# GpSimd's split of the experts' down weights, one tile sooner inside a feed-forward stage

## The chip, the cores and the metric

The program runs on one core of a Trainium2 chip. The metric is the device time of one execution in microseconds, as the median of a few runs; the profile is that of one execution. PE is TensorE, DVE VectorE, ACT ScalarE, POOL GpSimd and SP the engine that here issues transfers.

## The reference, cut to what matters

Input x is 8 x 256 x 512. Four blocks follow each other, each added to x: a convolution with 8-wide heads, a feed-forward block with quantised activations and ternary weights, an attention over a context, and a mixture of 16 experts (two routed per token) with two shared ones. The change touches the second block's stage:

```
def _bitlinear(x, w, b):
    xn = _layer_norm(x)
    xq = _activation_quant(xn)          # round(x * 127 / max|x|), per row
    wq = _weight_quant(w)               # -1, 0, 1 times a scale
    return einsum('bsd,fd->bsf', xq, wq) + b
h = _bitlinear(x, w1, b1)               # 512 -> 2048
h = gelu(h, approximate=False)
return _bitlinear(h, w2, b2)            # 2048 -> 512
```

It also touches a piece of preparation for the fourth block: that block's down weights `L1_ffn_rw2` (16 experts, 256 x 512 float32) are used as two bf16 parts, a high part (the value rounded to bf16) and a low part (the float32 difference to it).

## The kernel before, in words

The program is a row of stages; inside a stage each engine has its own instruction stream and the streams meet at semaphores. A stage ends for all engines together. The feed-forward stage is `stage_ffn` (L784). It takes 16 tiles of 128 tokens through a pipeline; every engine runs steps n = -3 ... 17, and different parts of a step belong to different tiles.

- PE, `up` (L1087): for tile t 16 matmuls of 512 columns into `ps_fH`, and four for the bias; `down` (L1111): 16 matmuls into `ps_fY`, once the transposed rounded rows (`f_qbT`) are there.
- ACT: `gelu` (L1000) reads `ps_fH` in two halves into `f_h`; `square` (L1010) sums squares and forms the variance; `scale` (L1018) multiplies by the quantiser.
- DVE: `centre` (L916) subtracts the mean (L919, 128 x 2048), `farthest` (L921) takes the largest magnitude (L923), `scale_of` (L925) needs that and the inverse root (L929 to L932), `round_h` (L934) rounds to bf16 (L938) and raises `qb_ready`, `add_y` (L942) adds the projected tile to the residual (L946). It also quantises the tile three further on (L605, L606). At the end it forms the low parts of keys and values for the next stage (L951, L955, L960), between the last two additions.
- SP, L884 to L891: for each e from 0 to 15 in program order: transpose of the quantised input of tile e + 3 (`turn_qa`, L871), transpose of the rounded rows of tile e (`turn_qb`, L877), wait for expert e's low part, store its two parts to DRAM (L889), load the raw weights of expert e + 2 (L851, 512 KB, waits that buffer e % 2 was split). The first two loads go out at the stage's start. A DMA waiting at the head of SP's stream holds back those behind it.
- POOL, L1066 to L1076: one inverse root for 12 tiles' input scales (L578), then the inverse root of tile 0 (`inverse_root`, L1050, L1052, one column). After that a loop over n: wait until tile n is rounded, cast expert n's weights to bf16 (`down_high`, L1059; waits for its load and for the store of expert n - 2, which used the same buffer), inverse root of tile n + 1, the difference for expert n (`down_low`, L1064), and for the last four n a bias addition on one tile of the residual (`add_bias2`, L1048, for tiles 0 to 3).

All orders are written out by hand; there is no planner. The four functions of POOL that are named here use no PSUM. The stored parts are read again only in the fourth block, hundreds of microseconds later.

Of the kernel before, what the change touches and what calls it, by code (L numbers as in the profile page):

```python
# [18 lines left out]
NT = TOK // P  # L19
# [764 lines left out]
def stage_ffn(k, scales, b1_parts, b2, ahead, quantised):  # L784
# [3 lines left out]
    with ExitStack() as ctx:  # L788
# [23 lines left out]
        rstd_ready, centred, quant_ready, h_scaled, qb_ready = (sem(n) for n in ("rstd", "cent", "quant", "hsc", "qb"))  # L812
# [229 lines left out]
        @block.gpsimd  # L1042
        def _(pool):
            pool.memset(ahead.rows[:, :], 0.0).then_inc(rows_zeroed, 1)

            def add_bias2(t):
                pool.wait_ge(y_added, t + 2)
                pool.tensor_tensor(tile(t), tile(t), b2[:, :].unsqueeze(1), ALU.add)  # L1048

            def inverse_root(t):  # L1050
                pool.wait_ge(var_ready, t + 1)
                pool.tensor_tensor(col(t % 2, RSTD), col(t % 2, VAR), k.pow_half[:, 0:1], ALU.pow).then_inc(rstd_ready, 1)  # L1052

            def down_high(e):
                p = e % 2
                pool.wait_ge(d_loaded[p], 16 * (e // 2 + 1))
                if e >= 2:
                    pool.wait_ge(d_stored[p], 16 * (e // 2))
                pool.tensor_copy(d_parts[p][:, 0, :], d_raw[p][:, :]).then_inc(d_high, 1)  # L1059

            def down_low(e):
                p = e % 2
                pool.wait_ge(d_high, e + 1)
                pool.tensor_tensor(d_parts[p][:, 1, :], d_raw[p][:, :], d_parts[p][:, 0, :], ALU.subtract).then_inc(d_low, 1)  # L1064

            pool.wait_ge(others_var, 1)  # L1066
            scales.inverse_root(k, pool, OTHER_TILES).then_inc(others_rstd, 1)
            inverse_root(0)
            for n in range(NT):
                pool.wait_ge(qb_ready, n + 1)  # L1070
                down_high(n)
                if n + 1 < NT:
                    inverse_root(n + 1)
                down_low(n)
                if n >= NT - AHEAD * TPB:
                    add_bias2(n - (NT - AHEAD * TPB))  # L1076
# [1993 lines left out]
```

## Time and profile before

| what | value |
|---|---|
| median of 3 runs | 1163.91 us (1163.27 to 1166.69) |
| profiled execution | 1166.8 us, its span 1165.1 us |
| mean granted TensorE clock of the span | 0.94 |
| PE busy | 1051.7 us (90%) |
| DVE busy | 881.9 us (76%) |
| ACT busy | 697.4 us (60%) |
| POOL busy | 603.2 us (52%) |
| feed-forward stage | from 230.25 us to about 371.0 us of the span |

A busy time is the time in which the engine worked on some instruction. Timeline lines give start, duration, engine, line, operation, tiles written and read, and in square brackets how long the engine had been idle and what ended that. PEld is the loading of weights into TensorE, SPq the issuing of a transfer on SP's queue. A DMA's landing is later than its issue.

### The profile page before, as it was taken

How to read it: one execution, taken by the hardware profiler on the slowest of the kernel's cores; microseconds unless marked ns; L12 is line 12 of the kernel's file. 1: busy time of each engine (PE TensorE's matmuls, PEld its weight loads, DVE VectorE, ACT ScalarE, POOL GpSimd, SP SyncE). 2: the span in 40 equal slices, each digit the busy share in tenths (PEclk: the TensorE clock that was granted, in tenths of full speed). 3: DMA queues.
4: the chain of work that ended last, by engine and by line, in shares of the span. 5: the costliest groups of instructions: out<-in, count | busy, mean ns of one | idle time of the engine just before them, and what ended most of it. 6: DMA issues, size and time to landing. Idle time of an engine off the chain costs nothing. (4 is left out here: it accounts for less than half of the span.)

```text
span 1165.1 us, 24953 instructions
## 1 busy us (share of the span) xinstructions
PE 1051.7 (90%) x9247; PEld 781.0 (67%) x9247; DVE 881.9 (76%) x1610; ACT 697.4 (60%) x1135; POOL 603.2 (52%) x637
## 2 busy tenths in 40 slices
PE   5899997689997899778999989698997899999995
PEld 5677776534444567456777766497774788888883
DVE  5589998879998987667888888588966555555538
ACT  4564772889985556367888876385444354454530
POOL 4444446334454733357888887313685355555510
PEclk9999998799999999978999999658999899999998
DMA  8573531879886013222222220385796477778878
GB/s 312 191 253 110 167 101 41 157 212 227 223 223 186 24 61 109 83 63 56 56 56 57 56 56 2 108 332 184 194 267 229 160 235 241 242 233 286 318 269 302
DMA packets 133819, 194.63 MB, mean 167 GB/s; under 512 B 68102, under 2 KB 70316, under 8 KB 132904
## 3 DMA queue, kind: packets, MB, share of 16 engines
q1 hardware_dynamic: 117368, 149.45, 42.3%
q0 software_dynamic: 8544, 24.68, 6.9%
q10 hardware_dynamic: 7792, 18.96, 5.1%
q8 instruction: 72, 1.18, 0.4%
q14 instruction: 43, 0.35, 0.1%
HBM read 127.47 MB, written 44.48 MB: 148 GB/s over the span
## 5 line engine op out<-in xcount | busy, mean ns | idle before, releaser
L470 PE MATMUL ps_y<-kv,toep 128*128 128x288 f32 x640 | 156.7, 407 | 3.4 <-DMA toep<-taps_padded 2.3
L470 PEld LDWEIGHTS ps_y<-kv,toep 128*128 128x128 f32 x640 | 121.1, 190 | 38.4 <-DMA toep<-taps_padded 4.1
L1679 POOL TENSOR_TENSOR vw<-at_pf,kw 128x1024 bf16<-128x1024 f32 x64 | 136.4, 2132 | 2.7 <-ACT kw L1739 2.7
L164 POOL TENSOR_TENSOR kv<-kx 128x1024 f32<-128x1024 f32 x32 | 60.6, 1893 | 84.2 <-DVE outT L524 37.8
L2665 POOL DMA_INDIRECT expert_results<-e_yo,target x47 | 69.8, 1484 | 55.5 <-ACT e_yo L2712 55.5
L1735 ACT ACTIVATE at_pf<-ps_st 128x1024 f32<-128x1024 f32 x64 | 65.5, 1023 | 39.4 <-PE ps_st L1875 35.7
L1786 DVE TENSOR_REDUCE at_negmax<-ps_s 128x4 f32<-128x1024 f32 x64 | 78.4, 1225 | 2.5 <-PE ps_s L1836 0.6
L1147 PEld LDWEIGHTS ps_eg<-e_xT,e_w 128*128 128x128 bf16 x1128 | 69.0, 100 | 14.9 <-DVE e_w L2766 2.5
L1147 PE MATMUL ps_eg<-e_xT,e_w 128*128 128x128 bf16 x1128 | 73.1, 223 | 4.0 <-DVE e_xT L2773 4.0
L1147 PE MATMUL ps_eu<-e_xT,e_w 128*128 128x128 bf16 x1128 | 72.3, 222 | 0.0
L2766 DVE COPY e_w<-expert_weights 128x4096 bf16 x47 | 57.7, 1227 | 18.4 <-issue 18.4
L2779 DVE SCALAR_TENSOR_TENSOR e_y<-ps_eu,e_bias,e_y 128x128 f32<-128x128 f32 x94 | 28.7, 347 | 54.8 <-PE ps_eu L1147 54.1
L2660 POOL DMA_INDIRECT e_rows<-token_rows,token x45 | 43.5, 968 | 51.1 <-PE ps_ex L2866 45.2
L1739 ACT ACTIVATE kw<-at_pf 128x1024 bf16<-128x1024 f32 x64 | 67.6, 1057 | 2.0
L1100 PE MATMUL ps_fH<-w1T,f_qaT 128*128 128x512 bf16 x256 | 63.7, 393 | 3.8 <-PEq L636 2.3
L1147 PEld LDWEIGHTS ps_eu<-e_xT,e_w 128*128 128x128 bf16 x1128 | 66.6, 99 | 0.0
L1780 DVE COPY qs<-ps_m 32x256 bf16<-32x256 bf16 x128 | 37.6, 293 | 36.8 <-PE ps_m L1848 33.8
L1116 PE MATMUL ps_fY<-w2T,f_qbT 128*128 128x512 bf16 x256 | 59.4, 387 | 4.2 <-DMA f_qbT<-f_qb 4.2
L2728 ACT ACTIVATE e_xT<-ps_ex 128x512 bf16<-128x512 bf16 x47 | 28.1, 597 | 58.0 <-PE ps_ex L2866 58.0
L494 DVE TENSOR_TENSOR prod<-ps_y,qx 128x1024 f32<-128x1024 f32 x32 | 39.2, 1224 | 23.1 <-ACT ps_y L417 23.1
L1147 PE MATMUL ps_ed<-e_parts,e_yhi 128*128 128x512 bf16 x188 | 55.9, 379 | 0.4 <-DVE e_ylo L2787 0.4
L2721 ACT ACTIVATE e_y<-ps_eg,e_bias 128x128 f32<-128x128 f32 x94 | 29.4, 363 | 40.3 <-PE ps_eg L1147 31.9
(444 smaller groups left out, 3052.8 us busy)
## 6 DMA issues: line engine op xcount, KB each, us to landing
e_parts<-down_parts SPq DMA_DIRECT2D x47, 512.0 KB, 4.5
w_raw<-in_L_ffn_w ACTq DMA_DIRECT2D x32, 512.0 KB, 4.4
toep<-taps_padded SPq DMA_DIRECT2D x32, 256.0 KB, 3.5
f_draw<-in_L_ffn_rw SPq DMA_DIRECT2D x16, 512.0 KB, 4.6
down_parts<-f_dparts SPq DMA_DIRECT2D x16, 512.0 KB, 2.9
expert_weights<-expert_results SPq DMA_DIRECT2D x16, 512.0 KB, 9.6
x_res<-in_x SPq DMA_DIRECT2D x4, 1024.0 KB, 11.3
c_in<-in_ctx SPq DMA_DIRECT2D x4, 1024.0 KB, 14.3
```

The source lines that it names most:

```text
L164: pool.tensor_tensor(pairs[:, :, :, 0:HD0], x[:, :, 0:HD0].unsqueeze(2).broadcast_to([P, ROWS_N, WIDE, HD0]), sliding_rows(x, 0, 1, WIDE), ...
L470: last = pe.matmul(y[:, l * B:(l + 1) * B, :, WIDE - 1:], toep[h % 2][:, (DC - 1 - l + m) * P:(DC - l + m) * P], kv[h % 2][:, m * B:(m + 1 ...
L1100: pe.matmul(psH[:, f, :].rearrange("p (a t) -> p a t", t=P), qaT[p][:, c, :], k.w1T[:, f * DC:(f + 1) * DC, c, :], start=(c == 0), stop=False)
L1116: last = pe.matmul(psY[p][:, :].rearrange("p (a t) -> p a t", t=P), qbT[p][:, c, :], k.w2T[:, :, c, :], start=(c == 0), stop=(c == FC - 1))
L1147: instruction = pe.matmul(out, stationary[a], moving[b], start=first and n == 0, stop=last and n == 2)
L1679: pool.tensor_tensor(pl[u % 4][:, :, :, :], pf[u % 2][:, :, :, :], ph[u % 4][:, :, :, :], ALU.subtract)\
L1735: act.activation(pf[u % 2][:, :, :, :], psT[:, :, :, :], ACT.Exp, scale=SCORE_SCALE).then_inc(exped, 1)
L1739: act.activation(ph[u % 4][:, :, :, :], pf[u % 2][:, :, :, :], ACT.Copy).then_inc(p_high, 1)
L1786: dve.tensor_reduce(negmax[u % 2][:, :].rearrange("p (j q) -> p j q", j=2), psS[:, :, :, :], AX.X, ALU.max, negate=True).then_inc(max_read, 1)
L2660: pool.indirect_dma_start(out=rows[j % 2], out_offset=None, in_=k.scratch["rows"], in_offset=bass.IndirectOffsetOnAxis(ap=token[:, j:j + 1 ...
L2665: pool.indirect_dma_start(out=k.scratch["results"], out_offset=bass.IndirectOffsetOnAxis(ap=target[:, j:j + 1], axis=0), in_=yo[j % 2], in ...
L2766: dve.tensor_copy(w1[j % 2][:, :, :, :].rearrange("p h c f -> p (h c f)"), W[:, bass.ds(e, 1), :, :, :].rearrange("p o h c f -> p (o h c f ...
```

## The change

The first split (cast and difference of expert 0) is placed directly behind the inverse root of tile 0, with no wait for a rounded tile. The loop runs over n from 1; round n waits for tile n - 1 to be rounded, casts expert n, takes the inverse root of tile n and forms the difference of expert n. The bias additions keep their condition on n. SP's order is not touched.

```diff
             inverse_root(0)
-            for n in range(NT):
-                pool.wait_ge(qb_ready, n + 1)
+            down_high(0)
+            down_low(0)
+            for n in range(1, NT):
+                pool.wait_ge(qb_ready, n)
                 down_high(n)
-                if n + 1 < NT:
-                    inverse_root(n + 1)
+                inverse_root(n)
                 down_low(n)
                 if n >= NT - AHEAD * TPB:
                     add_bias2(n - (NT - AHEAD * TPB))
```

NT is 16 and AHEAD * TPB is 4.

## Rows read from the trace of the kernel before

**Rows 1.** Engine time by stretch: stretch, length, busy per engine, PEclk, DMA share, GB/s.
```profile
277.00:300.00 23.00, 23.00 (x108) 10.40 (x107) 22.02 (x35) 20.88 (x28) 10.90 (x9) 1.00 0.92 225
360.20:363.50 3.30, 3.30 (x10) 1.15 (x8) 3.30 (x3) 3.30 (x4) 2.48 (x2) 0.50 0.52 110
```

**Rows 2.** Timeline of TensorE's weight loads: first group of two successive tiles.
```profile
274.24 1.61 PEld L1100 LDWEIGHTS ps_fH<-w1T,f_qaT 128*128 128x128 bf16 x8
...
282.01 1.61 PEld L1100 LDWEIGHTS ps_fH<-w1T,f_qaT 128*128 128x128 bf16 x8
```

**Rows 3.** Timeline: rounding of two successive tiles, and a GELU that waits.
```profile
269.69 1.22 DVE L938 TENSOR_SCALAR f_qb<-f_h 128x2048 bf16<-128x2048 f32 x1
...
277.18 1.22 DVE L938 TENSOR_SCALAR f_qb<-f_h 128x2048 bf16<-128x2048 f32 x1
...
317.86 1.12 ACT L1007 ACTIVATE f_h<-ps_fH,f_sc 128x1024 f32<-128x1024 f32 x1 [0.35 <-PE ps_fH L1107]
```

**Rows 4.** SP's queue in one tile, the loads' landing, and DMA idle time.
```profile
L877 SPq DMA_TRANSPOSE f_qbT<-f_qb x16: 1516/1948/3358, 249.2 to 360.9; - x16
...
278.42 2.47 SPq L877 DMA_TRANSPOSE f_qbT<-f_qb  x1
282.12 0.34 SPq L889 DMA_DIRECT2D down_parts<-f_dparts  x1
282.52 0.43 SPq L851 DMA_DIRECT2D f_draw<-in_L_ffn_rw  x1
...
DMA to landing us min/median/max: 3.6/4.6/5.8
...
289.80:290.10 0.30, 0.30 (x3) 0.18 (x2) 0.30 (x1) 0.30 (x1) 0.00 (x0) 1.00 0.01 1
```

**Rows 5.** Timeline: GpSimd's round and VectorE's scale and centring beside it.
```profile
272.47 2.13 POOL L1064 TENSOR_TENSOR f_dparts<-f_draw,f_dparts 128x1024 bf16<-128x1024 f32 x1
...
274.08 1.60 DVE L919 TENSOR_SCALAR f_h<-f_h,f_sc 128x2048 f32<-128x2048 f32 x1
...
278.46 1.04 POOL L1059 CAST f_dparts<-f_draw 128x1024 bf16<-128x1024 f32 x1 [3.86 <-DVE f_qb L938]
...
279.46 0.54 POOL L1052 TENSOR_TENSOR f_sc<-f_sc,pow_half 128x1 f32<-128x1 f32 x1
...
280.63 0.21 DVE L929 TENSOR_SCALAR f_sc<-f_sc 128x1 f32<-128x1 f32 x1
...
281.89 1.29 DVE L919 TENSOR_SCALAR f_h<-f_h,f_sc 128x2048 f32<-128x2048 f32 x1
```

**Rows 6.** Timeline: GpSimd's first two casts.
```profile
249.14 1.04 POOL L1059 CAST f_dparts<-f_draw 128x1024 bf16<-128x1024 f32 x1 [6.88 <-DVE f_qb L938]
...
255.98 1.04 POOL L1059 CAST f_dparts<-f_draw 128x1024 bf16<-128x1024 f32 x1 [3.20 <-DVE f_qb L938]
```

**Rows 7.** Timeline: centrings without and with a bias addition beside them.
```profile
331.19 1.04 POOL L1059 CAST f_dparts<-f_draw 128x1024 bf16<-128x1024 f32 x1 [4.13 <-DVE f_qb L938]
...
334.90 1.29 DVE L919 TENSOR_SCALAR f_h<-f_h,f_sc 128x2048 f32<-128x2048 f32 x1
...
342.56 1.27 POOL L1048 TENSOR_TENSOR x_res<-x_res,ffn_b 128x512 f32<-128x512 f32 x1
342.68 2.24 DVE L919 TENSOR_SCALAR f_h<-f_h,f_sc 128x2048 f32<-128x2048 f32 x1
```

**Rows 8.** Timeline of the stage's end: TensorE's last projections, VectorE's last work.
```profile
358.99 5.30 PE L1116 MATMUL ps_fY<-w2T,f_qbT 128*128 128x512 bf16 x16 [3.15 <-DMA f_qbT<-f_qb]
...
360.79 1.22 DVE L951 TENSOR_TENSOR kv_c0lo<-ctxT,kv_c0hi 128x1024 bf16<-128x1024 f32 x1
361.93 2.06 DVE L955 TENSOR_TENSOR kw<-qs,kw 128x1024 bf16<-128x1024 f32 x1
...
365.33 3.61 PE L1116 MATMUL ps_fY<-w2T,f_qbT 128*128 128x512 bf16 x16 [1.04 <-DMA f_qbT<-f_qb]
...
366.97 3.35 DVE L960 TENSOR_TENSOR vw<-qs,vw 128x2048 bf16<-128x2048 f32 x1
...
370.25 0.74 DVE L946 SCALAR_TENSOR_TENSOR x_res<-ps_fY,f_out_scale,x_res 128x512 f32<-128x512 f32 x1
```

## The prediction

> **What bounds the kernel now.** I read the page first (the whole program keeps TensorE busy for nine tenths of its span), then the table of engine time by stretch for the feed-forward stage, which runs from 230 to 371 us, then the timeline of single tiles engine by engine, with SP's queue last. In the body of the stage TensorE has no gap at all and VectorE is busy 22.0 of 23 us, while GpSimd has only 10.9 of 23 [rows 1]. So GpSimd is not a bound in itself; what can matter is when its small inverse root comes, what its long operations do to VectorE, and when the transfers behind it run.
>
> Two clocks run side by side. TensorE starts the first matmul group of a tile every 282.01 - 274.24 = 7.77 us [rows 2]. The VectorE and ScalarE chain rounds a tile every 277.18 - 269.69 = 7.49 us [rows 3]. The chain is thus the faster one by 0.28 us a tile; it begins the stage behind and catches up, and the first row in which ScalarE waits for TensorE's projection (0.35 us) is at 317.86 [rows 3]. From there TensorE sets the pace, and four more tiles follow until 350 us. A delay of the chain is forgiven up to about 4 x 0.28 = 1.1 us, and what is more arrives in the tail. The tail (from 350 us) is one tile's latency: centring, maximum, scale, rounding, the transposing DMA, the last down-projection 365.33 to 368.94, and the last add, 370.25 to 370.99 [rows 8].
>
> **The change part by part.** GpSimd's instructions stay the same in number, so I ask only what moves.
>
> 1. The first split. GpSimd idles for 6.88 us ahead of 249.14, so from 242.26 [rows 6]. The cast (1.04 us) and the difference (2.13 us) [rows 5] fit: 3.17 us, done by about 245.5. Expert 0's load was issued at the stage's start. VectorE has little but columns of one element in that time. Cost 0; the next root is due only after 249 us. If the cover were gone the price would be at most these 3.17 us.
>
> 2. The body. The n-th round now waits for the rounding of tile n - 1, which is the event that released the round before it, and issues cast, root, difference in the same order. Root n therefore hangs on the same event as before. Only the expert's number is one higher. Nothing is gained: the root ends at 279.46 + 0.54 = 280.00 and VectorE's first use is at 280.63, behind its own reduction [rows 5], so 0.6 us of slack were already there.
>
> 3. The transfers. SP takes, for each tile, the transposing DMA of the rounded rows, then the store of the split weights, then the load of the expert two further on. Before, the store waited for GpSimd: issued at 282.12, and the load at 282.52, which is 3.70 and 4.10 us behind the transpose's issue at 278.42 [rows 4]. Now the split is done a tile earlier, so store and load follow the transpose's own issue (median 1.95, at most 3.36 us). But the load's consumer comes a whole tile sooner: load e + 2, issued behind transpose e, is wanted when tile e + 1 is rounded, 7.49 + 0.04 = 7.53 us after transpose e was issued. Before, it was wanted 15.0 us after. The landing: issue to landing is 3.6/4.6/5.8 us [rows 4]. If nothing queues, it lands 1.95 + 0.4 + 4.6 = 7.0 us after the transpose's issue, 0.5 us in time. If the DMA engines are the limit, only their idle gap ahead of the store can be won; it is 0.6 us (289.80 to 290.40, share 0.01 in the first half [rows 4]), so 4.10 + 4.6 - 0.6 = 8.1 us, 0.6 us late. If nothing is won, 8.7, which is 1.2 us late. I take 7.8: the engines are busy for 0.92 of the time [rows 1], so nearer to the queued case. That is 0.3 us late.
>
> The Trainium skill's page "DMA: Bandwidth & Descriptors", section "Queues, rings and completion order", says that on each DMA engine descriptors are consumed in ring order, so an earlier store only queues behind the transpose; by that rule the landing would be the 8.1 us case and the sum below about 1 us larger. The idle gap of 0.6 us is what the trace shows of it; no row shows a store queued.
>
> What 0.3 us costs: the root has 0.6 us of slack, so nothing there. But GpSimd's difference then ends 0.3 us later and lies longer over VectorE's centring. Where it overlaps that by 0.5 us (272.47 + 2.13 = 274.60 against a start at 274.08) the centring takes 1.60 us, where it overlaps by 0.2 us 1.29 [rows 5]. So 0.3 us for a late tile; as landings scatter to both sides I take half, 0.15 us a tile, for 11 tiles 1.65 us. The first such load is worse: the interval from 249.14 to 255.98 is only 6.84 us [rows 6], so it is 0.9 us late, of which 0.6 is hidden; with the overlap I take 0.6 us. Sum 2.25, less the 1.1 forgiven: **+1.15 us** in the tail. Bounds: 0 (all land in time), and rival B below.
>
> 4. The bias adds. They hang on n >= 12, so each of the four comes one tile sooner: three before lie beside a later tile's work and one at the very end; now one lands behind the difference of the round that starts at 331.19, from about 334.8 to 336.1. VectorE's centring at 334.90 takes 1.29 us today; the next one, which meets a bias add at 342.56, takes 2.24 us [rows 7]. So +0.95 us on VectorE, once, and only part of ScalarE's later waits for TensorE (0.35 to 0.8 us) takes it up, because GpSimd's own work moves with the chain and overlaps the two next centrings longer. I carry it as **+0.9 us**; bounds 0 and 1.4.
>
> The Trainium skill's page "SBUF — State Buffer", section "Who interferes with whom", says that GpSimd and a VectorE operation in a two-port mode exclude each other for the whole instruction; by that rule the centring would wait for 336.1 and cost 1.2 us in place of 0.95. The row at 342.68 agrees in kind.
>
> 5. The tail. After the last rounding (360.87) GpSimd had a cast, a difference and a bias add; all are gone. VectorE's two key differences took 2.06 us each, its value difference 3.35, while the batch's difference of the same size as a key half took 1.22 just before [rows 8]. Uncontended I put them at 1.2, 1.2 and 2.3 (twice the elements). The last add then no longer waits behind the value difference (370.32) but for TensorE's end at 368.94: 369.0 + 0.74 = 369.7 against 370.99, **-1.27 us**. The first key half's gain goes nowhere, as the add after it waits for TensorE at 364.3. The last store goes out earlier and was not last anyway. All engines pass into the next stage at this end, and TensorE starts there at once, so a shift of the end is passed on.
>
> The sum: +1.15 + 0.9 - 1.27 = +0.8 us. The profiled execution took 1166.8 us (span 1165.1, 1.7 around it), 2.9 above the median of the three runs, so it would become 1167.6, and the median 1163.9 + 0.8 = **1164.7 us**.
>
> **Rivals.** About 0.3%, or 3.5 us, is what a measurement of this kernel tells from no change.
>
> A, all hidden: loads land in time, and the chain's waits absorb the extra bias add. For it: ScalarE waits for TensorE in the last body tiles. Against: VectorE's 22.0 of 23 us. Then only the tail counts: 1163.9 - 1.3 = 1162.6 us.
>
> B, slower: the loads set the pace. The place is the cast that waits for a load in each round; the price is that cast, root and difference all shift, and the centring waits them out. It decides once a load lands more than 0.6 us late at the 7.49 us cycle. With the landing at 8.7 us the cycle P settles where the delay equals the lateness: P = 7.49 + (8.7 - P), so 8.1 us, 0.6 more for each of 12 tiles, 7.2 us. Less 1.1, plus 0.9, minus 1.3: +5.7, 1169.6 us. For it: the load's landing of up to 5.8 us. Against: its issue surely comes sooner, and the engines do have a gap.
>
> C, the clock: the down-projection of tile 14 ran from 358.99 for 5.30 us, the last for 3.61 [rows 8], with a granted clock of 0.50 from 360.20 to 363.50 [rows 1], after TensorE had starved for 3.15 us. If the shifted tail puts both down-projections into the low stretch: +0.8 + 1.7 = 1166.4; if neither, about 1163.0.
>
> D, the change does not do what it says: it does split sooner, but nobody waits for the split but the store, so this coincides with the forecast.
>
> **Chances.** Forecast 0.48 (own range 1163.4 to 1166.3), A 0.24, B 0.16, C 0.12. Only an unforeseen shift in the later stages gives over 3.5 us of gain. Faster 0.08, within 0.74, slower 0.18 (B and a bad C). The range for 8 in 10 is 1161.9 to 1168.6.
>
> **What would show it.** In the changed profile: a cast near 242.3 us and none behind the last rounding; the casts of the body waiting for the load's DMA instead of the rounded tile, and loads issued about 2.4 us behind the transpose; centrings around 1.4 to 1.6 us, and one near 335 us at 2.2; VectorE's value difference at 2.3 us and the last add set free by TensorE. The step on transfers is wrong if no cast waits for a DMA; the step on bias adds if the end of the last centring is not later relative to the stage's start; the forecast as a whole if the stage's length changes by over 2.5 us.

## The result and the profile after

The changed kernel is slower: 1171.86 us (median of 8 runs, 1169.63 to 1176.4) against 1164.55 us for the kernel before on the same chips (8 runs, 1162.93 to 1168.75). The ratio is 1.0054, 95% interval 1.0035 to 1.0072, so +6.3 us (+4.1 to +8.4). It lies above the forecast range; the rival with the load as pacemaker, which I had put at 0.16, is what happened, at about its price (+5.7).

The page of the kernel after, its opening lines and the clock (the span of before was 1165.1 us, its POOL busy time 603.2):

```profile
span 1169.1 us, 24952 instructions
## 1 busy us (share of the span) xinstructions
PE 1055.2 (90%) x9247; PEld 778.4 (67%) x9247; DVE 884.6 (76%) x1610; ACT 698.0 (60%) x1135; POOL 602.3 (52%) x637
...
PEclk9999998799998999978999999758999899999998
```

The instructions are the same and GpSimd's busy time did not grow, so somebody waits. The stage is measured from its first load's issue to the first load of the next stage: 371.26 - 230.25 = 141.0 us before, 376.74 - 229.25 = 147.5 us after. These 6.5 us are the size of the whole loss, and what GpSimd waited for tells where they arise. (The two profiled spans differ by 4.0 us only: outside the stage this execution of the changed kernel was 2.5 us shorter.) The waits of the kernel after in the stage (engine and line, releaser, us in total, times, longest), the loads' landing times, and the engine times of a stretch that answers to [rows 1]:

```profile
POOL f_dparts L1059 <- DMA f_draw<-in_L_ffn_rw: 37.1, 9, 5.5
POOL f_dparts L1059 <- DVE f_qb L938: 21.7, 6, 3.9
```

```profile
DMA to landing us min/median/max: 3.8/5.2/6.0
```

```profile
276.00:299.00 23.00, 22.47 (x105) 9.85 (x102) 21.68 (x33) 19.00 (x24) 10.32 (x9) 1.00 0.79 202
```

Nine of GpSimd's casts now end their wait with the load, none did before. Loads land 5.2 us after their issue in place of 4.6 [rows 4]. TensorE, without a gap in this part before, has one (22.47 of 23 us).

One tile of it in SP's queue, on GpSimd and on VectorE, kernel after:

```profile
265.16 1.77 SPq L877 DMA_TRANSPOSE f_qbT<-f_qb  x1
266.98 1.15 SPq L889 DMA_DIRECT2D down_parts<-f_dparts  x1
268.18 0.44 SPq L851 DMA_DIRECT2D f_draw<-in_L_ffn_rw  x1
...
272.65 2.52 SPq L877 DMA_TRANSPOSE f_qbT<-f_qb  x1
275.22 0.57 SPq L889 DMA_DIRECT2D down_parts<-f_dparts  x1
275.85 0.43 SPq L851 DMA_DIRECT2D f_draw<-in_L_ffn_rw  x1
```

```profile
274.33 1.04 POOL L1059 CAST f_dparts<-f_draw 128x1024 bf16<-128x1024 f32 x1 [5.49 <-DMA f_draw<-in_L_ffn_rw]
275.32 0.54 POOL L1052 TENSOR_TENSOR f_sc<-f_sc,pow_half 128x1 f32<-128x1 f32 x1
275.82 2.13 POOL L1064 TENSOR_TENSOR f_dparts<-f_draw,f_dparts 128x1024 bf16<-128x1024 f32 x1
281.82 1.04 POOL L1059 CAST f_dparts<-f_draw 128x1024 bf16<-128x1024 f32 x1 [3.86 <-DVE f_qb L938]
```

```profile
271.41 1.22 DVE L938 TENSOR_SCALAR f_qb<-f_h 128x2048 bf16<-128x2048 f32 x1
...
275.99 0.21 DVE L929 TENSOR_SCALAR f_sc<-f_sc 128x1 f32<-128x1 f32 x1 [1.17 <-POOL f_sc L1052]
...
276.93 2.11 DVE L919 TENSOR_SCALAR f_h<-f_h,f_sc 128x2048 f32<-128x2048 f32 x1
280.54 1.22 DVE L938 TENSOR_SCALAR f_qb<-f_h 128x2048 bf16<-128x2048 f32 x1
...
285.25 1.29 DVE L919 TENSOR_SCALAR f_h<-f_h,f_sc 128x2048 f32<-128x2048 f32 x1
288.03 1.22 DVE L938 TENSOR_SCALAR f_qb<-f_h 128x2048 bf16<-128x2048 f32 x1
```

Read it from the top. The load went out 268.18 - 265.16 = 3.0 us behind its transpose (4.1 before [rows 4]; I expected 2.4) and the cast began 9.2 us behind the transpose, while the rounding that releases the cast when the load is there was over at 272.63. So the cast is 1.6 us late, the root with it, and VectorE has nothing to do for 1.17 us at L929, where its slack had been 0.6 us [rows 5]. The difference then ends at 277.95, over the centring, which takes 2.11 us in place of 1.3. Together the cycle from rounding to rounding is 9.13 us. The next one is 7.49 us again: the long cycle gave the next load time. This tile is the worst but one: over the nine casts that waited for their load, the cast is 0.2 to 2.0 us late, 1.0 in the median, and begins 7.7 to 9.2 us behind the transpose, 8.6 in the median. The stage goes on mostly in such pairs, and from the first to the last rounding (247.59 to 366.09) the mean cycle is 7.90 us, against 359.65 - 247.85 over the same 15 cycles, 7.45 us, before.

Two costs add up on VectorE. In the whole stage it waits for the root 5.3 us in seven places, against 0.7 us in one before, and its 16 centrings take 27.1 us in place of 24.3. Between 250 and 352 us, where it never waited for the root before, the changed kernel has:

```profile
DVE f_sc L929 <- POOL f_sc L1052: 4.3, 5, 1.4
```

The tail of the kernel after, VectorE then TensorE (compare [rows 8]):

```profile
366.09 1.35 DVE L938 TENSOR_SCALAR f_qb<-f_h 128x2048 bf16<-128x2048 f32 x1 [1.38 <-ACT f_h L1021]
367.36 1.21 DVE L951 TENSOR_TENSOR kv_c0lo<-ctxT,kv_c0hi 128x1024 bf16<-128x1024 f32 x1
368.50 1.22 DVE L955 TENSOR_TENSOR kw<-qs,kw 128x1024 bf16<-128x1024 f32 x1
...
373.51 2.28 DVE L960 TENSOR_TENSOR vw<-qs,vw 128x2048 bf16<-128x2048 f32 x1
375.71 0.75 DVE L946 SCALAR_TENSOR_TENSOR x_res<-ps_fY,f_out_scale,x_res 128x512 f32<-128x512 f32 x1
```

```profile
365.44 6.22 PE L1117 MATMUL ps_fY<-w2T,f_qbT 128*128 128x512 bf16 x16 [4.24 <-DMA f_qbT<-f_qb]
371.90 3.61 PE L1117 MATMUL ps_fY<-w2T,f_qbT 128*128 128x512 bf16 x16 [0.23 <-DMA f_qbT<-f_qb]
```

VectorE's differences take 1.22 and 2.28 us in place of 2.06 and 3.35: that part of the change works. From the first rounding to the last it is 359.65 - 247.85 = 111.8 us before and 118.5 after, 6.7 us more; from the last rounding to the end it is 371.26 - 359.65 = 11.6 us before and 10.65 us after, 1.0 us less. That makes +5.7 us from the first rounding on. The other 0.7 us of the stage's 6.5 lie ahead of the first rounding (17.6 us before, 18.3 after), and most of that is no effect of the change: the profile of before_warm, a kernel that is the kernel before up to its tail, has 18.1 us there. Its TensorE ran the stage's start longer at the low one of its two levels (1.2 GHz; the high one is 2.4): mean granted clock 0.61 over 232.7 to 234.7 us, against 0.87 over the same two microseconds of the stage (233.3 to 235.3) in the profile of before. From the first rounding on the two agree (123.4 us).

### The profile page after: what moved, and what is told of

Read it like the earlier page. It is cut to its first block and busy times, and to the rows that moved or that the text cites. A ratio compares the mean times of both kernels' runs of the same rounds, so it can differ in the third digit from the quotient of the medians.

```text
span 1169.1 us, 24952 instructions
## 1 busy us (share of the span) xinstructions
PE 1055.2 (90%) x9247; PEld 778.4 (67%) x9247; DVE 884.6 (76%) x1610; ACT 698.0 (60%) x1135; POOL 602.3 (52%) x637
## 6 DMA issues: line engine op xcount, KB each, us to landing
x_res<-in_x SPq DMA_DIRECT2D x4, 1024.0 KB, 11.6
```

## The experiments

Each experiment was timed beside the kernel before, in three groups on different chips; the gains in us below are the ratio times that group's time of the kernel before. "Stage" is measured as above, in the one profiled execution; the clock at the stage's start alone moves it by about half a microsecond. The ratio is the test of the time.

| kernel | ratio to before (95%) | stage us |
|---|---|---|
| changed kernel | 1.0054 (1.0035 to 1.0072) | 147.5 |
| sp_shift | 0.9986 (0.9972 to 0.9999) | 141.5 |
| load_first | 1.0047 (1.0028 to 1.0066) | 146.0 |
| root_first | 1.0023 (1.0009 to 1.0036) | 143.6 |
| load_aside | 0.9987 (0.9973 to 1.0000) | 140.2 |
| late_loads | 1.0111 (1.0089 to 1.0133) | 156.9 |
| half_loads | 0.9987 (0.9975 to 0.9999) | 140.8 |
| shift_bias_late | 1.0008 (0.9992 to 1.0023) | 144.7 |
| shift_bias_end | 1.0011 (0.9996 to 1.0026) | 143.1 |
| shift_load2 | 0.9983 (0.9969 to 0.9996) | 141.2 |
| load_ahead | 0.9984 (0.9971 to 0.9997) | 140.3 |
| before_warm | 1.0012 (0.9994 to 1.0030) | 141.6 |
| shift_load2_warm | 0.9989 (0.9974 to 1.0003) | 141.0 |

**Is it the loads? Take the wait away (load_aside), or give the loads their tile back (sp_shift).**

```diff
+                if e >= 2: place = rows of "results" in DRAM, written again later
-                pool.wait_ge(d_loaded[p], 16 * (e // 2 + 1))
+                pool.wait_ge(d_loaded[p], 16)
```

> The changed kernel, but the loads of experts 2 to 15 go to DRAM rows that are written again later, and GpSimd splits the raw weights of experts 0 and 1 over and over, so that it waits for no load; the stored parts of experts 2 to 15 are thus those of 0 and 1. Issue order and the bytes read are those of the changed kernel. Theory 1: without the wait the body runs as before, about -0.4 us against before (-1.3 to +0.5). Theory 3 (crowded DMA engines): the loss stays, +5 to +6 us. Theory 2: +6 us.

```diff
+            store_and_load(0)
             for e in range(E_N):
                 ...
                 turn_qb(e)
-                (wait, store e, load e + 2)
+                (wait, store e + 1, load e + 3)
```

> The changed kernel, with SP's stores and loads moved one expert sooner as well: the store of expert e + 1 and the load of expert e + 3 follow the transpose of tile e and wait for the split as in the kernel before, so that each load has two tiles until it is wanted. Theory 1 (late loads hold the cast and what is queued behind it): no cast waits for a DMA, the body runs as before, and what is left is the tail's gain of 1.3 us and the bias addition's cost of up to 0.9, so -0.4 us against before (-1.3 to +0.5). Theory 2 (the bias additions one tile sooner are the cost): it stays at about +6 us, as they are where the change put them. Theory 3 (store and load issued at once behind the transpose crowd the DMA engines and make the transposes land late): also about -0.4, since they are issued as late as before.

Both came out a little better than the best that was expected (-1.3 us): -1.5 us (0.9987) and -1.6 us (0.9986). The difference to the changed kernel is about 8 us, and load_aside has the same issue order, reads the same bytes, and its transfers land as late as the changed kernel's (5.2 us after their issue). So the waiting for the loads is the loss, and neither the bias additions nor crowded transposes are. In sp_shift every cast in the stage is released by VectorE again; its waits between 250 and 352 us:

```profile
POOL f_dparts L1065 <- DVE f_qb L944: 51.8, 14, 4.2
```

Its tail (same columns as before) shows the gain that the change is able to give. The last add waits for TensorE, not for the value difference:

```profile
360.40 1.23 DVE L944 TENSOR_SCALAR f_qb<-f_h 128x2048 bf16<-128x2048 f32 x1 [1.38 <-ACT f_h L1027]
...
365.61 2.28 DVE L966 TENSOR_TENSOR vw<-qs,vw 128x2048 bf16<-128x2048 f32 x1
369.71 0.75 DVE L952 SCALAR_TENSOR_TENSOR x_res<-ps_fY,f_out_scale,x_res 128x512 f32<-128x512 f32 x1 [1.82 <-PE ps_fY L1123]
```

From the last rounding to the next stage's first load (370.75) it takes 10.35 us, 1.26 us less than before.

**How much load is too much? Half the bytes (half_loads), and the loads alone cut short (late_loads).**

```diff
-                load F2 = 2 blocks of rows
+                parts = F2 if e < 2 else 1     # load this many
```

> The changed kernel with loads of experts 2 to 15 of half the bytes (256 KB; the other half of the raw buffer keeps what experts 0 and 1 left, so half of the stored parts are not theirs). Theory 1: the transfer's packets take 1 to 1.5 us less, the landing falls from about 9.0 us behind the transpose's issue to 7.7 to 8, so the casts are late by under 0.6 us and the root's slack hides that: -0.5 to +2 us against before. If lateness does not matter, +6 us.

With a landing of 3.5/3.8/4.6 us (min/median/max), in the median 1.4 us less than in the changed kernel, no cast waits for a DMA, and the loss is gone whole (0.9987, -1.5 us, better than the -0.5 to +2 that I expected). So 1.4 us of landing time are enough to win the whole loss back.

```diff
 # kernel before, SP, behind store e
-                if e + 2 < E_N:
-                    load(e + 2)
+                if 1 <= e < E_N - 1:
+                    load(e + 1)
```

> The kernel before, where only the loads are cut short of time: behind the store of expert e goes the load of expert e + 1 in place of e + 2 (first behind store 1), so that each load has one tile less until it is wanted; GpSimd's order and the store's wait are those of before. Theory 1 (a load that is wanted about one tile after it was issued arrives late, and the cast, the root and the difference behind it move): slower by +5 to +9 us, more than the changed kernel's 6.3, since load and store also wait for the split, while the tail's 1.3 us is not gained. If the loss of the changed kernel came from the bias additions, from the tail or from stores issued at once (theories 2 and 3), this kernel loses nothing: within 1 us of before.

This is the kernel before with nothing but one tile less for the loads, and it loses twice as much as the changed kernel: +13 us (10.4 to 15.5), well above the 5 to 9 that I expected. Here each load also goes out behind the wait for the split, and the split is late because of the load, so lateness feeds itself: the casts of two successive rounds lie 277.73 - 267.88 = 9.85 us apart. The profile names no releaser for these waits ("issue"); the loads were issued 5.1 and 5.8 us ahead of the casts, and the landings of this kernel's loads take 3.7 to 5.7 us, so the load fits as what they wait for.

```profile
262.83 0.43 SPq L851 DMA_DIRECT2D f_draw<-in_L_ffn_rw  x1
...
271.95 1.57 SPq L851 DMA_DIRECT2D f_draw<-in_L_ffn_rw  x1
```

```profile
267.88 1.04 POOL L1059 CAST f_dparts<-f_draw 128x1024 bf16<-128x1024 f32 x1 [5.48 <-issue]
...
277.73 1.04 POOL L1059 CAST f_dparts<-f_draw 128x1024 bf16<-128x1024 f32 x1 [6.20 <-issue]
```

**Through what does a late load cost? The root ahead of the wait (root_first).**

```diff
+                inverse_root(n)
                 pool.wait_ge(qb_ready, n)
                 down_high(n)
-                inverse_root(n)
                 down_low(n)
```

> The changed kernel, with GpSimd's inverse root of tile n ahead of the wait for the rounded tile and of the cast, so that a late load no longer holds the root. Loads land as late as in the changed kernel. Theory 1a (the price is the root that is queued behind the waiting cast): most of the loss goes, +1 to +2 us against before. Theory 1b (the price is GpSimd's late difference beside VectorE's centring): the loss stays, +4 to +6 us. Theories 2 and 3: +6 us.

+2.7 us (1.0 to 4.2), between the two theories: somewhat more than half of the changed kernel's loss goes, the rest stays. VectorE's waits for the root in the body are gone (0.7 us in one place in the whole stage, as before). So both ways are real, and by the medians the root behind the cast is the larger. What stays is consistent with the late difference beside the centring: the 16 centrings take 27.8 us in sum, against 24.3 in the kernel before, and their median is 1632 ns here and 1409 ns there:

```profile
L919 DVE TENSOR_SCALAR f_h<-f_h,f_sc x16: 1286/1632/2623, 237.9 to 352.7; 128x2048 f32<-128x2048 f32 x16
```

That remainder was not taken apart further.

**Can the order of store and load save it (load_first)?**

```diff
+                if e + 2 < E_N:
+                    load(e + 2)
                 sp.dma_start(down_parts e ...)
-                if e + 2 < E_N:
-                    load(e + 2)
```

> The changed kernel, with the load of expert e + 2 issued ahead of the store of expert e. Theory 1: the store's packets take 1.7 us of the DMA engines ahead of the load, so the load lands about 1.7 us sooner, 7.4 us behind the transpose's issue in place of 9.1, which is in time or nearly: 0 to +1.5 us against before. Theory 3 (crowded transposes): the same bytes in the same place, so it stays at +6 us. Theory 2 (bias additions): +6 us.

My forecast was wrong: 1.0047, hardly better than the changed kernel. The load is in time now, but the cast has a second DMA to wait for, the store of the expert two before it, which empties the buffer that the cast fills. Its waits between 250 and 352 us:

```profile
POOL f_dparts L1059 <- DMA down_parts<-f_dparts: 38.6, 9, 4.8
POOL f_dparts L1059 <- DVE f_qb L938: 15.3, 4, 3.9
```

Whichever of the two stands second in the queue is late. So the shortened time is the pair's, not the load's alone.

**Only the loads ahead (load_ahead), and a gentler start (shift_load2).**

```diff
+                if e and e + 2 < E_N:
+                    load(e + 2)
                 turn_qa(e + 3)
+                if e == 0: load(2)
                 turn_qb(e)
                 sp.wait_ge(d_low, e + 1)
                 (store e)
-                if e + 2 < E_N:
-                    load(e + 2)
```

> The changed kernel with one thing moved: each load goes ahead of the two transposes of its round in place of behind them (load 2 between them), which the earlier split allows, since its buffer is free by then; the stores stay at once behind the transpose. Theory 1 (only the loads' lateness costs): no cast waits for a DMA, -1 to -1.6 us against before. Theory 3 (transfers ahead of the transposes, or stores at once behind them, delay the rounded rows and with them the last projections): 0 to +3 us.

0.9984, -1.9 us, a little better than theory 1 said. No cast waits for a DMA. The early split frees the raw buffer a tile sooner, so the load may go ahead of the transposes; the changed kernel had left it behind them.

```diff
+            load(2)
             for e in range(E_N):
                 turn_qa(e + 3)
                 turn_qb(e)
+                if e == 0: store(0)
-                (store e, load e + 2)
+                (store e + 1, load e + 3)
```

> SP's stores and loads moved one expert sooner as in sp_shift, but ahead of the transpose for tile 3 goes only the load of expert 2; the store of expert 0 goes behind the first transpose of rounded rows. In sp_shift TensorE waited 1.9 us for that input transpose (1.15 in the kernel before), as store 0 and load 2 lay ahead of it in the queue. Theory 4 (what is ahead of a transpose on the DMA queue delays the stage's start): the wait falls back towards 1.2 us, 0.4 to 0.7 us better than sp_shift, so -1.8 to -2.3 us against before. If TensorE's wait there is made up later: -1.6 us, as sp_shift.

0.9983: the wait of TensorE's weight load for an early quantised input fell from 1.9 to 0.9 us, but the time does not differ from sp_shift's (intervals overlap almost wholly). The three versions that give the loads their time are all faster than before by 1.6 to 2.0 us, with intervals that just exclude 1; shift_load2 has the lowest ratio. I don't rank them.

**The bias additions (shift_bias_late, shift_bias_end).**

```diff
 # sp_shift; late:
-                if n >= NT - AHEAD * TPB: add_bias2(n - (NT - AHEAD * TPB))
+                if n > NT - AHEAD * TPB: add_bias2(n - 1 - (NT - AHEAD * TPB))
+            add_bias2(AHEAD * TPB - 1)
 # end: all four behind pool.wait_ge(qb_ready, NT)
```

> The kernel with SP's stores and loads moved too (-1.6 us against before), with each bias addition one round later, so beside the tiles where it lay before, and the last one behind the last difference. Theory 2b (the extra bias addition beside a centring costs 0.75 to 0.95 us on VectorE, and the last add waits for TensorE by 1.8 us, which hides a bias addition there): -2.3 to -2.6 us against before. If the bias additions' place is worth nothing: -1.6 us as without.

> The same, with all four bias additions behind the last rounding. The two that lay beside the last centrings (2.24 and 2.28 us each in place of 1.29) go from the chain, so up to 1.9 us more; the four then take 5.1 us or more beside VectorE's key and value differences, whose slack ahead of the last add is 1.8 us. Theory 2b: -2.5 to -4 us against before if the differences are hidden, about -2 if they push the last add out. If the bias additions' place is worth nothing: -1.6 us.

Both expectations failed: 1.0008 and 1.0011, by the ratios 2.6 to 2.9 us worse than sp_shift, where I expected better; the ratios are from two chips and their intervals overlap a little. The body is not what differs: from the rounding of tile 11 to that of tile 15 it is 29.75 us before, 29.5 in sp_shift, 29.75 in shift_bias_late and 29.5 in shift_bias_end. So the sooner additions cost the chain nothing. sp_shift's centrings of tiles 13 to 15:

```profile
335.87 2.23 DVE L925 TENSOR_SCALAR f_h<-f_h,f_sc 128x2048 f32<-128x2048 f32 x1
...
344.06 1.55 DVE L925 TENSOR_SCALAR f_h<-f_h,f_sc 128x2048 f32<-128x2048 f32 x1
...
351.42 1.29 DVE L925 TENSOR_SCALAR f_h<-f_h,f_sc 128x2048 f32<-128x2048 f32 x1
```

The first meets the new addition and takes 2.23 us, as the price in [rows 7] says; but the two later ones, 2.24 and 2.28 us before, get shorter, because the delayed VectorE no longer lines up with GpSimd in the same way: there GpSimd's additions take 2.26 and 2.35 us, where they took 1.27 before. In shift_bias_late the last centring takes 2.29 us again. Its loss lies behind the last rounding's start: 12.95 us to the next stage's first load, against 10.35 in sp_shift. The last rounding meets the last additions (2.12 us in place of 1.23), and the last down-projection takes 5.30 us in place of 3.61, at a mean granted clock of 0.66, where sp_shift has 1.00:

```profile
363.77 2.12 DVE L944 TENSOR_SCALAR f_qb<-f_h 128x2048 bf16<-128x2048 f32 x1 [1.38 <-ACT f_h L1027]
```

```profile
363.10 5.30 PE L1124 MATMUL ps_fY<-w2T,f_qbT 128*128 128x512 bf16 x16 [3.15 <-DMA f_qbT<-f_qb]
370.35 5.30 PE L1124 MATMUL ps_fY<-w2T,f_qbT 128*128 128x512 bf16 x16 [1.96 <-DMA f_qbT<-f_qb]
```

The two lengthenings are 0.9 and 1.7 us, together the 2.6. Whether the low clock there comes in every execution, one profile can't say. In shift_bias_end the four additions lie beside VectorE's key and value differences; the value difference takes 3.35 us again and the last add comes behind it, which gives 11.46 us in place of 10.35.

**The clock in the tail (before_warm, shift_load2_warm).**

```diff
             def down(t, p):
+                if known(t) and t >= NT - 2:
+                    pe.wait_ge(gelu_done, 2 * NT)
+                    (12 matmuls for tile 14, 10 for tile 15, into psH, which nobody reads any more)
```

> The kernel before, with 12 matmuls ahead of the down-projection of tile 14 and 10 ahead of that of tile 15, into a PSUM tile that nobody reads, so that TensorE does not starve in the tail; they change no result. Theory C (the low clock near 360 us costs): the down-projection of tile 14 takes 3.6 us in place of 5.3, but the last one starts when its transposed rows land (365.3), so the stage gains 0 to 0.3 us; against before -0.5 to +0.3 us. If the low stretch also carried into what follows: -1 to -2 us.

> shift_load2 with the same added matmuls. Theory C: without a low stretch at the stage's end in any run, 0 to 1 us better than shift_load2 (whose down-projections may fall into one), -1.8 to -3 us against before. If the low stretch does not matter: as shift_load2.

1.0012 and 0.9989: no gain, if anything a little worse. In before_warm the down-projection of tile 14 does take 3.61 us in place of 5.30, but the last one starts when its transposed rows land, at 365.30 us against 365.33. A low clock at tile 14 is therefore hidden. And the last down-projection takes 3.61 us, the time at the high clock, before, in the changed kernel and in sp_shift alike, so the clock in this tail does not separate these three. It counts only where it reaches the last one, as in shift_bias_late.

## Why the prediction was wrong

*Which step failed.* Part 3, the landing of the loads. I bounded it at 7.0 to 8.7 us behind the transpose's issue, on the thought that an earlier issue can win nothing or something, but not lose, and took 7.8. Measured, the casts that waited for their load began 8.6 us behind it in the median, and 9.2 in the tile shown: in effect nothing was won by the earlier issue. Two terms were mis-sized. The gap between the transpose's issue and the load's is 3.0 us (2.9 to 3.6 over the stage), not 2.4: a store issued on the heels of a transpose keeps SP for 1.15 us here, 0.6 to 1.3 over the stage, in place of 0.34. And the landing time, 4.6 us, was taken from loads issued 4.1 us behind the transpose; issued 3.0 us behind it they take 5.2, up to 6.0. I had computed that 0.6 us of lateness is hidden by the root's slack; the real 1.6 us is over it by 1.0, and VectorE stands idle by 1.17 us at just that place. For the whole body I had +1.15 us, net of the 1.1 us that the chain could make up; from the first rounding to the last it is 6.7 us longer.

*What I had for it and did not use.* The profile said that the DMA engines are busy for 0.92 of the time, and that the trade is one tile of lead (7.5 us) against an issue at most 2 us earlier. With a landing spread of 3.6 to 5.8 us that was never safe; rival B had the mechanism, the place and, at +5.7 us, nearly the price, though not the shape: it has every cycle 0.6 us longer, and the runs show a long one and a short one in turn, 0.45 us longer in the mean. Its chance of 0.16 and a range that ended below it were the mistake. The 1.1 us that the chain could make up was too small to matter.

*The rule on ring order* (descriptors are consumed in ring order: the Trainium skill's page "DMA: Bandwidth & Descriptors", section "Queues, rings and completion order") was my case of 8.1 us. It pointed the right way, and the measured median of 8.6 us is later still. But load_aside and load_ahead show that order by itself costs nothing; what costs is that the wanted time came first.

*Part 1 (first split) and part 2 (body order)* held. The first cast ran at 241.95, behind the first root, and nothing shows a delay by it; the root hangs on the same event whenever the load is there.

*Part 4 (bias additions)* was wrong in what it sums to. One centring costs 0.95 us more, as said, but later ones give it back. From the rounding of tile 11 to the last one sp_shift and load_aside take 29.5 us and load_ahead 29.9, against 29.75 before: no cost, where I had 0.9. The step that failed is that GpSimd's own work, moving with the chain, would overlap the two next centrings longer; they became shorter.

*Part 5 (tail)* held in sp_shift: 1.27 us forecast, 1.26 measured; 1.0 in the changed kernel.

*Rival C (clock)* shows in long down-projections of tile 14, 5.30 us before and 6.22 after, but they are hidden: the last one takes 3.61 us in both, and the added matmuls gained nothing.

What stays open: the versions with the loads in time are 1.6 to 2.0 us faster than before by their ratios, while sp_shift's profiled stage is 0.5 us longer than that of before. Part of this is the start of the stage, where the profile of before has the higher clock. From the first rounding to the end it is 123.4 us before, 122.9 in sp_shift, 123.0 in load_ahead and 121.95 in load_aside. The tail's 1.2 to 1.3 us are in all three. But the body of sp_shift and load_ahead takes 0.7 to 0.8 us more than that of before: in sp_shift the chain runs at TensorE's pace, 7.78 us a tile, from tile 7's rounding on, before only from tile 10's; in load_ahead the first cycle takes 7.76 us in place of 6.85. Where the rest of their measured gain lies, one profile of each can't say.

## What to carry to other kernels

When work is pulled forward, pull its inputs as well: a consumer that moves one tile sooner takes a whole tile from its transfers, however much sooner they may be issued, and a busy queue gives back little of it. Check both DMAs that a double-buffered step waits for, the one that fills its input and the one that empties its output, and look at what is queued behind the waiting instruction; here a tiny operation behind it carried somewhat more than half of the loss. A cost beside another engine's work, taken from one row, does not add up over tiles: it shifts the alignment of the next ones.

## What the runs showed of the hardware that was not expected

A plain store issued right behind a DMA transpose kept SP's queue for 1.15 us (0.6 to 1.3 over the stage), against 0.34 us when it went out 3.7 us after the transpose's issue. The shorter the transpose's own issue, the longer the store's: 1.77 and 1.15 us in one tile, 2.52 and 0.57 in the next. A pair of transfers that is issued sooner into a busy queue landed later after its issue: loads 5.2 us in place of 4.6, and stores 3.2 to 4.2 against 2.6 to 3.0 (each counted from the start of the issue, so the longer issue is in it). And GpSimd's and VectorE's operations that read two tiles slow each other: in the tail of before GpSimd's difference of 2.13 us took 2.98 and VectorE's of 1.22 us 2.06, and none of it remained where GpSimd was idle.
